# Second attention of a two-layer kernel: causal masks of the key scores by a GpSimd select, value sums of a step in one run

## What is computed

```python
q, k = _apply_rope(q, k, sin, cos)
att = jnp.einsum('bhtd,bhsd->bhts', q, k) * scale
causal = jnp.tril(jnp.ones((T, T), dtype=bool))
att = jnp.where(causal[None, None], att, -jnp.inf)
att = jax.nn.softmax(att, axis=-1)
y = jnp.einsum('bhts,bhsd->bhtd', att, v)
```

## Time and profile before

| | |
|---|---|
| runs | 4164.34 us median of 3 (4151.19 to 4166.54) |
| profiled execution, first to last instruction | 4106.3 us (no device time is listed for this execution itself; the span is 58.0 us under the median) |
| PE busy | 85% |
| DVE busy | 70% |
| ACT busy | 43% |
| POOL busy | 18% |
| granted TensorE clock, mean | 0.924 of full speed |

### The profile page before, as it was taken

The page is one execution under the profiler, slowest core; times in us unless marked ns, Lnnn a source line. Parts: engine busy times, 40 slices in busy tenths (PEclk is TensorE's granted clock), DMA queues, the critical chain, the costliest instruction groups (busy, mean ns, idle before and its releaser), DMA issues. The chain is left out here.

```text
span 4106.3 us, 65569 instructions
## 1 busy us (share of the span) xinstructions
PE 3499.3 (85%) x20499; PEld 1877.5 (46%) x20500; DVE 2863.1 (70%) x5100; ACT 1766.9 (43%) x2274; POOL 745.4 (18%) x968
## 2 busy tenths in 40 slices
PE   5777777777359999999999999999997999999954
PEld 2333333343113333333333333333335888888943
DVE  5777776776468777788778778787724665566556
ACT  2333333333103665666566566566673332233211
POOL 0333323233112222100000000000002121111066
PEclk9899888888658999999999999999998999999977
DMA  2121221212232221123333212223002121121077
GB/s 70 45 79 57 67 83 41 82 51 68 78 75 45 48 47 35 25 41 47 48 46 48 48 26 41 39 41 48 7 7 90 58 71 61 66 67 62 32 204 215
DMA packets 261897, 247.41 MB, mean 60 GB/s; under 512 B 92530, under 2 KB 233970, under 8 KB 261306
## 3 DMA queue, kind: packets, MB, share of 16 engines
q1 hardware_dynamic: 245178, 209.58, 21.8%
q0 software_dynamic: 16384, 33.64, 2.8%
HBM read 149.70 MB, written 92.67 MB: 59 GB/s over the span
## 5 line engine op out<-in xcount | busy, mean ns | idle before, releaser
L1313 DVE TENSOR_REDUCE at_part<-at_p 128x1 f32<-128x512 f32 (+3 forms) x2560 | 1402.1, 605 | 310.4 <-PE at_p L1197 192.2
L1294 ACT ACTIVATE at_ex<-at_st 128x1024 f32<-128x1024 f32 (+1 forms) x1280 | 1109.3, 895 | 830.8 <-PE at_st L1220 472.5
L1197 PE MATMUL at_p<-at_ks,at_qs 96*128 96x512 bf16 (+3 forms) x2560 | 838.3, 366 | 89.6 <-DVE at_part L1313 32.8
L1217 PE MATMUL at_st<-at_qs,at_ks 99*128 99x512 bf16 (+3 forms) x2560 | 713.3, 350 | 6.5 <-ACT at_ex L1294 4.9
L1234 PE MATMUL at_ob<-at_ex,at_vs 128*32 128x512 f32 (+3 forms) x5120 | 588.3, 541 | 3.6 <-ACT at_ex L1294 3.5
L1197 PEld LDWEIGHTS at_p<-at_ks,at_qs 96*128 96x128 bf16 x2560 | 248.1, 98 | 688.5 <-DVE at_part L1313 490.4
L1475 POOL DMA_INDIRECT e_xg<-s_xn,e_table x128 | 146.9, 1148 | 1978.2 <-DMA e_table<-s_table 1405.2
L1565 ACT ACTIVATE e_hh<-e_hb,e_b1now 128x512 fp32r<-128x512 f32 x256 | 176.3, 689 | 527.5 <-PE e_hb L1500 498.9
L1217 PEld LDWEIGHTS at_st<-at_qs,at_ks 99*128 99x128 bf16 x2560 | 242.0, 99 | 252.2 <-ACT at_ex L1294 97.8
L1530 PE MATMUL e_ob<-e_w2h,e_hh 128*128 128x256 f32 x1024 | 295.1, 288 | 15.5 <-DVE e_og L1623 15.5
L1532 PE MATMUL e_ob<-e_w2h,e_hl 128*128 128x256 f32 x1024 | 291.7, 285 | 0.0
(11 more groups left out here) (180 smaller groups left out, 4706.9 us busy)
## 6 DMA issues: line engine op xcount, KB each, us to landing
s_qk<-a_piece SPq DMA_DIRECT2D x192, 128.0 KB
at_qs<-s_qk SPq DMA_DIRECT2D x192, 128.0 KB
at_ks<-s_qk SPq DMA_DIRECT2D x192, 128.0 KB
s_v<-a_v SPq DMA_DIRECT2D x64, 256.0 KB, 5.5
at_vs<-s_v SPq DMA_DIRECT2D x32, 512.0 KB
e_w<-w SPq DMA_DIRECT2D x16, 1024.0 KB, 7.5
s_eo<-e_og SPq DMA_DIRECT2D x32, 512.0 KB, 2.6
a_x<-x SPq DMA_DIRECT2D x16, 512.0 KB, 5.2
```

The costliest lines, as they stand in the source:

```text
L1197: last = pe.matmul(out, qs[0:STACK, r, h, qt * P:(qt + 1) * P], ks[0:STACK, r, h, ch * SEG:ch * SEG + w], start=True, stop=not diag)
L1217: last = pe.matmul(out, ks[:, r, h, kt * P:(kt + 1) * P], qs[:, r, h, q0:q0 + w], start=True, stop=not diag)
L1294: ev.done(act.activation(ex[:, u % NE, 0:width], st[:, u % 2, 0:width], ACT.Exp, scale=SCALE), "ex")
L1313: ev.done(dve.tensor_reduce(part[:, at, ch:ch + 1], p1[:, n % NP1, 0:w], AX, ALU.max), "mx")
```

## The change

1. `key_scores` no longer adds `mask_k`: 64 matmuls per group, 1024 in all, are gone from PE. In their place POOL runs `affine_select` on `ex` behind each exp of a unit on the diagonal: it sets the entries above the diagonal to 0. A unit of a step 0, 4, 10 or 18 takes two selects (one over two blocks of 128 columns, one over one), a unit of a step 1, 5, 11 or 19 takes one, 48 selects per group, 768 in all. `values` of such a step waits for a new semaphore, `causal`.
2. `values` of step s-1 is made in one run behind unit 3 of step s, instead of in two behind units 1 and 3.
3. The 64 scatters of the routing table move: they now stand in POOL's list behind the last step of each query chunk, four per group, and so last as long as the attention.

```diff
@@ -1021,7 +1021,6 @@
         ident = sb("ident", [P, P])
         identb = sb("identb", [P, P], BF16)
         mask_q = sb("mask_q", [P, P], BF16)
-        mask_k = sb("mask_k", [P, P], BF16)
         qs = sb("qs", [ROWS, NBUF, G, M], BF16)
         ks = sb("ks", [ROWS, NBUF, G, M], BF16)
         vs = sb("vs", [P, NBUF, NQT, G * HW])
@@ -1054,6 +1053,16 @@
             steps.append((qc, [(first + 2, 0, SEG - 2 * P)]))
         NS = len(steps)
         NU = NS * G
+
+
+        def on_diagonal(s):
+            qc, tiles = steps[s]
+            places = [at for kt, at, _ in tiles if kt >= TT * qc]
+            return [places[:2], places[2:]] if len(places) == 3 else [places] if places else []
+
+        def causal_until(u):
+            return sum(len(on_diagonal(x // G)) for x in range(u + 1))
+
         last_of = [max(s for s in range(NS) if steps[s][0] == qc) for qc in range(SPB)]
         chunks = [(h, qt, ch) for h in range(G) for qt in range(NQT) for ch in range(qt // TT + 1)]
         NC = len(chunks)
@@ -1070,7 +1079,7 @@
             return [n for n in range(NC) if due_at[n] == u]
 
         counts = dict(s1=NC, mx=NC, neg=1, negT=1, mT=1, m_in=PIECE, st=NU, ex=NU, pv=NS, oc=SPB, ot=SPB,
-                      norm=SPB, y_out0=SPB // 2, y_out1=SPB // 2, rden=SPB)
+                      norm=SPB, y_out0=SPB // 2, y_out1=SPB // 2, rden=SPB, causal=sum(len(on_diagonal(u // G)) for u in range(NU)))
         for i in range(NBUF):
             counts[f"in{i}"] = 1
         NLOAD = 2 * 12 + 2
@@ -1101,7 +1110,7 @@
             def _(sp):
                 route.load(sp)
                 for out, in_ in ((ident[:], io["c_ident"]), (identb[:], io["c_identb"]),
-                                 (mask_q[:], io["c_mask_q"]), (mask_k[:], io["c_mask_k"])):
+                                 (mask_q[:], io["c_mask_q"])):
                     sp.dma_start(out, in_).then_inc(consts, 16)
                 for rows in (qs, ks):
                     for i in range(NBUF):
@@ -1160,9 +1169,14 @@
             @block.gpsimd
             def _(pool):
                 pool.wait_ge(ready, 1)
-                route.wait_placed(pool)
-                def scatter(i):
-
+
+                def scatter(i, first):
+
+                    if first:
+                        route.wait_placed(pool)
+                    else:
+                        pool.wait_ge(scattered, 16 * TOPK * i)
+                        pool.sem_inc(passed, 1)
                     pool.tensor_copy(idx[:], keep["dest"][:, :, bass.ds(i, 1)].rearrange("p k o -> p (k o)")).then_inc(scat_copy, 1)
                     pool.tensor_copy(tok[:, 0:1], keep["token"][:, bass.ds(i, 1)]).then_inc(scat_copy, 1)
                     pool.wait_ge(scat_copy, 2 * i + 2)
@@ -1172,17 +1186,35 @@
                             out=dram["table"], out_offset=bass.IndirectOffsetOnAxis(ap=idx[:, k:k + 1], axis=0),
                             in_=tok[:, 0:1], in_offset=None).then_inc(scattered, 16)
 
-                scatter(0)
-                with pool.Fori(1, NT) as i:
-
-                    pool.wait_ge(scattered, 16 * TOPK * i)
-                    pool.sem_inc(passed, 1)
-                    scatter(i)
+
+                def only_before(g, u):
+                    places = on_diagonal(u // G)
+                    if places:
+                        ev.wait(pool, "ex", g, u + 1)
+                        pool.sem_inc(passed, 1)
+                    for at in places:
+                        if len(at) == 2:
+                            block = ex[:, u % NE, :].rearrange("p (b c) -> p b c", c=SEG)[:, :, 0:P]
+                            pattern = [[0, 2], [1, P]]
+                        else:
+                            block, pattern = ex[:, u % NE, at[0]:at[0] + P], [[1, P]]
+                        ev.done(pool.affine_select(block, block, pattern, ALU.is_ge, 0.0, 0, -1), "causal")
+
+                def group(g, first):
+                    for u in range(NU):
+                        only_before(g, u)
+                        if u % G == G - 1 and u // G in last_of:
+                            qc = last_of.index(u // G)
+                            scatter(g * SPB + qc, first and qc == 0)
+
+                group(0, True)
+                with pool.Fori(1, NGROUPS) as g:
+                    group(g, False)
                 pool.wait_ge(scattered, 16 * TOPK * NT)
 
             @block.tensor
             def _(pe):
-                pe.wait_ge(consts, 16 * (4 + 2 * NBUF))
+                pe.wait_ge(consts, 16 * (3 + 2 * NBUF))
                 pe.wait_ge(ready, 1)
 
                 def row_scores(g, r, n):
@@ -1211,32 +1243,28 @@
                     qc, tiles = steps[s]
                     ev.wait(pe, "ex", g, max(u - 1, 0))
                     for kt, at, w in tiles:
-                        diag = kt >= TT * qc
                         out = st[:, u % 2, at:at + w]
                         q0 = (qc + 1) * SEG - w
                         last = pe.matmul(out, ks[:, r, h, kt * P:(kt + 1) * P], qs[:, r, h, q0:q0 + w],
-                                         start=True, stop=not diag)
-                        if diag:
-                            last = pe.matmul(out[:, 0:P], identb[:], mask_k[:], start=False, stop=True)
+                                         start=True, stop=True)
                     ev.done(last, "st")
 
-                def values(g, r, s, half):
+                def values(g, r, s):
 
                     qc, tiles = steps[s]
-                    if half == 0:
-                        ev.wait(pe, "ex", g, G * s + G)
-                        if s == 0 or steps[s - 1][0] != qc:
-
-                            ev.wait(pe, "norm", g, qc)
-                    cut = (len(tiles) + 1) // 2
-                    for kt, at, w in tiles[:cut] if half == 0 else tiles[cut:]:
+                    ev.wait(pe, "ex", g, G * s + G)
+                    if on_diagonal(s):
+                        ev.wait(pe, "causal", g, causal_until(G * s + G - 1))
+                    if s == 0 or steps[s - 1][0] != qc:
+
+                        ev.wait(pe, "norm", g, qc)
+                    for kt, at, w in tiles:
                         for h in range(G):
                             last = pe.matmul(ob[h * HW:(h + 1) * HW, SEG - w:SEG], vs[:, r, kt, h * HW:(h + 1) * HW],
                                              ex[:, (G * s + h) % NE, at:at + w], start=(kt == 0),
                                              stop=(s == last_of[qc] and kt == tiles[-1][0]),
                                              skip_group_check=True)
-                    if half == (len(tiles) > 1):
-                        ev.done(last, "pv")
+                    ev.done(last, "pv")
 
                 def turn(g, qc):
                     ev.wait(pe, "oc", g, qc + 1)
@@ -1258,12 +1286,11 @@
                             row_scores(g + 1, (r + 1) % NBUF, n)
                         if more and u == TURN_AT + 1:
                             turn_maxima(g + 1)
-                        if h % 2 == 1 and s >= 1:
-                            values(g, r, s - 1, h // 2)
+                        if h == 3 and s >= 1:
+                            values(g, r, s - 1)
                         if h == 3 and s >= 1 and s - 1 in last_of:
                             turn(g, last_of.index(s - 1))
-                    for half in range(2):
-                        values(g, r, NS - 1, half)
+                    values(g, r, NS - 1)
                     turn(g, SPB - 1)
                     
                 route.prefix_sums(pe)
```

## The result

The changed kernel takes 4222.2 us in the median of 4 runs (4215.5 to 4227.1), the kernel before 4165.1 us beside it. The ratio is 1.0139, with a 95% interval of 1.0119 to 1.0159. It is slower by about 58 us (50 to 66 by the interval). The forecast was 4241 us, slower. Ratios are taken from fast runs: one run of all that follow, among the four of experiment 2, took 6874.6 us and is left out of them.

The account below looks back on a forecast made before the run. PE was taken to lead, tied to DVE by three PSUM buffers. +4.1 us per group (+62 in 15 groups), +12 for the last group and +3 for the last scatter gave +77: 4241 us, range 4110 to 4290.

Parts of the forecast that it names:

- What bounds: Second layer's attention: PE leads, DVE not far behind, their work tied by three PSUM buffers; the question is whether DVE stays fed.
- The masks: Key scores: 1024 mask matmuls, 56 us of PE, go; selects at 0.8 us per unit cost nothing on the path.
- Full steps: Nine steps per group without diagonal or turn: DVE idles behind the longer run, +0.33 us each, +3.0 per group.
- Steps with a turn: Steps 2, 6 and 12: sums, ACT's copy and transposes now follow one another while DVE gets nothing, +2.4 us per group.
- Diagonal steps: Steps 0, 1, 4, 5, 10, 11, 18 and 19: fewer masks, some new waits, together -1.3 us per group.
- The last group: Group without row scores: key scores wait for ACT's exps, full steps 5.2 us instead of 4.17, +12 us in all.
- The last scatter: End of the attention phase: the 64th scatter starts after the last select and ends later, +3 us.
- Rival 1: Whole attention: PE's list alone decides, all PE time saved comes through, some 4055 us; chance 0.16.
- Rival 3: Diagonal units: the select is late and POOL falls behind, +165 us, 4406 us; chance 0.05.
- Rival 2: Whole attention: the two parts cancel, full steps change by 0, a group by -0.4 us, 4173 us; chance 0.18.
- Adding the difference between span and median of the runs: Whole kernel: the profiled span lies 58.0 us under the runs' median, so +77 us was added to 4164.3.

Follow-up runs that it names:

- experiment 2: Kernel before with only the value sums of a step merged into one run behind unit 3; masks stay on PE: 4258.3 us, ratio 1.0199.
- experiment 5: DVE takes maxima over only half of each piece's columns, in both kernels: kernel before 4073.1 us (ratio 0.9774), changed kernel 4023.1 us (0.9654).
- experiment 4: Changed kernel without the selects and the wait on them, causal mask left out, scatters early again: 4239.3 us, ratio 1.0145.
- Experiment 3: Changed kernel with the sums of steps 1, 5 and 11 again behind unit 1 of the next step: 4200.5 us, ratio 1.0053.
- the hybrid: Changed kernel with full-step sums in two runs, large diagonal steps' sums in one behind unit 3, small ones' behind unit 1: 4123.1 us, ratio 0.9897.
- dve_half_after: Changed kernel with DVE taking maxima over only the first half of each piece's columns: 4023.1 us, ratio 0.9654.
- before_again: Kernel before, unchanged, run once more for a second profile: 4106.3 us.
- merge_only: Kernel before with only the value sums merged into one run behind unit 3: 4258.3 us, ratio 1.0199.

## Why the prediction was right

- **What bounds** held: PE leads, but through three buffers it can run ahead of DVE by three pieces only, and the merge broke that. Experiments 2 and 5 show it from both sides. A fourth buffer, which the prediction names as the other way out, was not tried.
- **The masks** were priced as hidden on POOL and worth their PE time only where PE sets the pace; experiment 4 shows the first, and the diagonal steps of experiment 5 speak for the second (3.5 us shorter per group, with 64 masks priced at 3.5 and four merged runs in them, against 1.3 with the whole reductions). Step 10 fell from 7.05 to 6.64 (6.65 by hand).
- **Full steps**: +0.33 each was too much. The four steps written out were right to within 0.02, but I took their mean for all nine. Read from the end of a step's last PE run to the end of the next step's, steps 3, 7, 8, 13 and 17 changed by +0.4, +0.3, +0.1, -0.1 and +0.1. The nine sum to +2.2 per group, not +3.0. Why these steps lose less was not looked into; they may have fewer columns, or their pieces may lie better over the units. 0.8 x 15 = 12 us is most of the 15 by which the forecast's 77 lies over the traces' 62.
- **Steps with a turn**: +0.5, +0.9 and +1.0, sum +2.4 as forecast. Experiment 3 gives 1.9 of it back.
- **Diagonal steps**: -1.35 in the same group against -1.3. Steps 18 and 19 were worse than I had them (+0.4 against +0.2), steps 0, 1, 5 and 11 a little off to either side.
- The group read so (1503.6 to 1621.1, against 1500.2 to 1614.5 before) grew by 3.2 us, as every plain group did; the mean over 15 groups is 3.0.
- **The last group** +13.4 against +12, by the chain through ACT that was named. The nine full steps cost 0.86 each, not 1.0, and the rest some 5.7 us, not 3: a sum that came out better than its terms. **The last scatter** +4.5 against +3.
- **Rival 1** fell, but the point from which it was to decide was put the wrong way. The prediction asks whether three buffers bridge the 2.28 us of run and restart, which a dearer reduction of 0.76 us would do. But that DVE runs dry is no loss in itself: in experiment 5 it stands 1.75 us behind a run, and the merge pays. What counts is whether DVE has time left in the step to catch up, and that comes with a cheaper reduction. At an estimated 0.34 us per 512 piece the change gains 50 us, about half of the 109 of rival 1. No run had a dearer one. **Rival 3** fell with the rows of the select. **Rival 2** had the parts cancelling; they don't, but the masks do take back some 30% of the merge's loss in a plain group (4.5 us to 3.2).
- Adding the difference between span and median of the runs was a weak step that did no harm. The 58 us were no launch cost (the changed kernel's span of 4225.3 belongs to a run of 4227.1) but the other level of the last phase.

## What to carry to other kernels

Merging short runs on a busy engine saves its switches, but count what the other engines hold in their buffers meanwhile: here three buffers of 0.6 us stood against a run of 1.85, and an estimated 56 us of saved switches became 83 us of loss. The question is not whether the neighbour runs dry behind a long run but whether it can catch up before the next: with halved reductions it did, and the same merge lost nothing over a whole group. Work placed behind a long run is hidden by it, so put long runs where something is late (the selects of diagonal steps) and short ones where a neighbour lives from hand to mouth. And write the step out from measured durations, for every kind of step: a mean over the steps that one happened to pick is the part that missed. Last, before two profiles are compared, look for stretches that no edit touched and that differ all the same.

## What the hardware showed

The negation of the maxima on DVE (fp32, SBUF to SBUF, 64 columns) takes longer in the changed kernel. The rows before and after:

```profile
L1319 DVE TENSOR_SCALAR at_negmax<-at_negmax x16: 195/196/213, 1259.6 to 3006.2; 128x64 f32<-128x64 f32 x16
```

```profile
L1346 DVE TENSOR_SCALAR at_negmax<-at_negmax x16: 196/358/359, 1260.9 to 3052.1; 128x64 f32<-128x64 f32 x16
```

On the timeline it lies inside a select of POOL's:

```profile
1496.04 0.65 POOL L1201 TENSOR_SCALAR_AFFINE_SELECT at_ex<-at_ex 128x256 f32<-128x256 f32 x2 [0.27 <-ACT at_ex L1321]
1496.14 0.36 DVE L1346 TENSOR_SCALAR at_negmax<-at_negmax 128x64 f32<-128x64 f32 x1
```

Without the selects it takes 0.19 us again (experiment 4), and in the hybrid too, where no select runs at that place. In the changed kernel the select of 256 columns starts 0.10 us before the negation and ends after 0.41, and the negation ends 0.05 us behind it; in dve_half_after, where the select starts 0.15 us before, the negation takes 0.305 us and ends 0.05 us behind it again. Without a select it is long too where an indirect DMA of POOL's runs beside it: once each in before_again (0.33 us) and merge_only (0.36 us). PE waits for it there, so it costs 0.16 us in 15 of 16 groups, about 2 us in all. The reductions, which read PSUM, keep their mean (685 ns before, 683 after). The Trainium skill (GPSIMD Engine Reference, Key points) says that GpSimd shares its SBUF interfaces with VectorE and that they contend where a DVE instruction is in a 2-port performance mode or has two SBUF inputs. These rows agree, if the negation runs in such a mode, which no row shows.

A select by a fixed pattern took 0.9 ns per column and some 0.18 us to start (0.29 and 0.41 us for 128 and 256 columns), well under the two-input add's 2.35 ns per element.
